# Sending expert outputs home by scatter instead of storing and gathering them, in a one-core attention and mixture-of-experts block

## The chip, the cores and the metric

The kernel runs on one core of a Trainium2 chip. The metric is the device time of one execution in microseconds, as a median over runs; less is better.

## What is computed

One transformer block over 4 x 1024 tokens of 128 features, all in float32. Its second half, a feed-forward with 16 experts of which each token uses one, beside a shared expert of 512 columns, is what the change touches.

```python
# x: (4, 1024, 128)
x = x + attention(layernorm(x))          # 16 heads of 8, no softmax: (q k^T / n^sigmoid(m)) v
h = layernorm(x).reshape(4096, 128)
logits = h @ router_w.T                  # 16 experts, top 1
score = sigmoid(top value), zero for the other experts
routed_in = h * score
gate, up = split(routed_in @ gate_up_proj[e])          # 128 -> 2 x 128
expert = (up * silu(gate)) @ down_proj[e]
shared = (silu(h @ shared_gate_w.T) * (h @ shared_up_w.T)) @ shared_down_w.T
x = x + shared + expert
```

## The kernel before

The 4096 tokens are 32 tiles of 128 rows; a group c is four of them (NQ = 8 groups). Token 128 t + p sits in partition p of tile t, in the residual `xres` and in the normed rows `h_rows`.

**Stages.** In the attention stage (`project`, `turn_q`, `v_by_k`, `attend` on TensorE) each group is projected, normed and added to the residual; `turn_h` and `route` give its router logits. On the vector engine `choose(c)` finds the top expert and `place(c)` the row of every token in the DRAM buffer `x_slots` (`pos`), in which each expert has a region with 128 rows of zeros ahead. GpSimd writes each tile's 128 rows there with an indirect DMA, `scatter(t)` (L353, issue at L358), 32 in all; a row is 128 features and the top logit, W = 129 words. When all are in, `slot_rows` and `take_table` make a table of 48 slots of 128 rows, each for one expert; slots that are not full reach into the zero rows or are not used.

**Expert stage**, in 12 groups g of four slots: SP loads the slots' rows (`load(g)`, L244, four DMAs at L251, first row from the table in registers); TensorE turns them (`turn_rows`), does gate and up (`gate_up_experts`), turns the product (`turn_act`) and does `down_experts`; ScalarE copies the result into the ring `yg` (`take_y`, L540, four buffers), and SP stores it to the DRAM buffer `y_slots` (`store(g)`, L253, issue at L255).

**The way back.** The vector engine works out where each token's y row lies (`y_rows`, L839 to L843, index `y_row`). When all twelve stores have landed, GpSimd gathers 32 tiles by that index into `h_rows` (L428 to L433), at most two under way (semaphores `back`). `add_experts(c)` (L858) waits for the four gathers of its group and for `add_shared(c)` and adds them to the residual (L863); SP stores the even groups and ScalarE's queue the odd ones (L285, L706).

**Shared expert.** 32 blocks n = 4 c + k of 128 of the 512 columns: `gate_up_shared(n)` (L1214, six matmuls, with `hT` split in a high and a low half), `silu_shared` on ScalarE (L517), `act_shared` on the vector engine (L850), `down_shared(n)` (L1224). The low half of group c is made on GpSimd by `hT_lo(c)` (L342, instruction at L344); block n waits for that of group n // 4 (`hT_rdy`, L1218). `add_shared(c)` adds a group's sum to the residual (L856).

**Order.** Every engine runs a list written out by hand, one call a line (SP from L258, GpSimd L361 to L433, ScalarE from L546, vector engine from L911, TensorE from L1278), and waits on semaphores in that order. TensorE's list mixes shared blocks into the expert stage: `gate_up_shared(10)` and `down_shared(9)` stand in it, and 11 to 31 follow it. On the vector engine the last calls are `add_shared(7)`, `add_experts(6)`, `add_experts(7)`.

Of the kernel before, what the change touches and what calls it, by code (L numbers as in the profile page):

```python
# [7 lines left out]
ALU = mybir.AluOpType  # L8
# [9 lines left out]
def build_block(nc, S, x, x_t, w_in, b_in, Wo, bo, m_col_in, router_t, gate_up, down, shared_gate, shared_up,  # L18
# [18 lines left out]
    W = D + 1  # L37
# [3 lines left out]
    YRING = 4  # L41
# [9 lines left out]
    y_slots = nc.dram_tensor("y_slots", (SLOTS * P, D), F32, kind="Internal").ap()  # L51

    with ExitStack() as ctx:
# [41 lines left out]
        from_slot = sb("from_slot", [P, NQ, Q])  # L95
        y_row = sb("y_row", [P, NT], I32)
# [56 lines left out]
        offs_all = sb("offs_all", [P, NQ, E, Q])  # L153
# [40 lines left out]
        y_st = [sem(f"y_st{i}") for i in range(YRING)]  # L194
        y_row_rdy = sem("y_row_rdy")
        back = [sem("back0"), sem("back1")]
# [6 lines left out]

        table_cols = table[:].rearrange("o a n -> o (a n)")
# [23 lines left out]
        def _(sp):  # L228
# [8 lines left out]
            sp.wait_ge(z_done, 1)  # L237
# [21 lines left out]
            load(0)  # L259
            load(1)  # L260
            load(2)
            load(3)
            load(4)
            load(5)
            load(6)
            load(7)
            load(8)
            store(0)
            store(1)
            load(9)  # L270
            store(2)
            load(10)
            load(11)
            store(3)
            store(4)
            store(5)
            store(6)
            store(7)
            store(8)
            store(9)  # L280
            store(10)
            store(11)
# [6 lines left out]
        def _(pool):  # L289
# [33 lines left out]
                   allow_small_or_imprecise_dtypes=True)  # L323
            g.iota(e_no[:], pattern=[[1, E]], base=0, channel_multiplier=0, allow_small_or_imprecise_dtypes=True)
# [3 lines left out]
                   allow_small_or_imprecise_dtypes=True).then_inc(k_ids, 1)  # L328

# [23 lines left out]
            def scatter(t):  # L353
                if t % Q == 0:
# [9 lines left out]
            scale_q(1)  # L364
            scale_q(2)
            scale_v(2)
            count(0)
            scale_v(3)
            scale_q(3)
            scatter(0)  # L370
            scatter(1)
            count(1)
            scatter(2)
            scatter(3)
            hT_lo(0)
            scale_v(4)
            scale_q(4)
            scatter(4)
            scale_v(5)
            scatter(5)  # L380
            scale_q(5)
            scatter(6)
            scatter(7)
            hT_lo(1)
            count(2)
            hT_lo(2)
            scale_v(6)
            scale_q(6)
            scatter(8)
            scatter(9)  # L390
# [3 lines left out]
            scatter(12)  # L394
            scatter(13)
            count(3)
            scatter(14)
            count(4)
            scatter(15)
            scale_q(7)  # L400
            scatter(16)
            scatter(17)
            scatter(18)
            scatter(19)
            hT_lo(3)
            scatter(20)
            scatter(21)
            count(5)
            scatter(22)
            scatter(23)  # L410
            count(6)
            scatter(24)
            scatter(25)
            scatter(26)
            scatter(27)
            count(7)
# [3 lines left out]
            scatter(31)  # L420
            hT_lo(4)
            hT_lo(5)
            hT_lo(6)
# [12 lines left out]
        def _(act):  # L436
# [103 lines left out]
            def take_y(g):  # L540
                act.wait_ge(e_dn_mm, g + 1)
                if g >= YRING:
                    act.wait_ge(y_st[g % YRING], 16 * (g // YRING))
# [3 lines left out]
            std_x(1)  # L547
            std_x(2)
            square(0)
            head_norms(0)  # L550
            square(1)
            weights_hi(0)
            std_x(3)
            weights_hi(1)
            head_norms(1)
            std_x(4)
            qT_copy(0)
            qT_copy(1)
            square(2)
            std_x(5)  # L560
            wb_copy(0)
            std_x(6)
            x1_copy(0)
            head_norms(2)
            std_h(0)
            norm_h(0)
            x1_copy(1)
            square(3)
            hT_copy(0)
            std_h(1)  # L570
            hT_hi(0)
            qT_copy(2)
            norm_h(1)
            head_norms(3)
            hT_copy(1)
            hT_hi(1)
            square(4)
            qT_copy(3)
            wb_copy(1)
            head_norms(4)  # L580
            x1_copy(2)
            square(5)
            std_h(2)
            head_norms(5)
            x1_copy(3)
            norm_h(2)
            std_h(3)
            hT_copy(2)
            qT_copy(4)
            hT_hi(2)  # L590
            std_x(7)
            norm_h(3)
            qT_copy(5)
            wb_copy(2)
            square(6)
            hT_copy(3)
            hT_hi(3)
            head_norms(6)
            x1_copy(4)
            square(7)  # L600
            silu_shared(0)
            silu_shared(1)
            std_h(4)
            head_norms(7)
            norm_h(4)
            x1_copy(5)
            hT_copy(4)
            hT_hi(4)
            std_h(5)
            silu_shared(2)  # L610
            qT_copy(6)
            wb_copy(3)
            silu_shared(3)
            norm_h(5)
            x1_copy(6)
            hT_copy(5)
            qT_copy(7)
            std_h(6)
            hT_hi(5)
            norm_h(6)  # L620
            x1_copy(7)
            hT_copy(6)
            hT_hi(6)
            std_h(7)
            norm_h(7)
            hT_copy(7)
            silu_shared(4)
            hT_hi(7)
            silu_shared(5)
            silu_shared(6)  # L630
            silu_shared(7)
            silu_shared(8)
            silu_shared(9)
            score_silu(0)
            rows_copy(0)
# [3 lines left out]
            score_silu(2)  # L639
            rows_copy(2)  # L640
            gate(1)
            score_silu(3)
            rows_copy(3)
            gate(2)
            take_y(0)
            score_silu(4)
            gate(3)
            score_silu(5)
            silu_shared(10)
            rows_copy(4)  # L650
            take_y(1)
            score_silu(6)
            rows_copy(5)
            score_silu(7)
            take_y(2)
            gate(4)
            score_silu(8)
            rows_copy(6)
            gate(5)
            take_y(3)  # L660
            rows_copy(7)
            score_silu(9)
            take_y(4)
            rows_copy(8)
            score_silu(10)
            gate(6)
            gate(7)
            take_y(5)
            score_silu(11)
            rows_copy(9)  # L670
            gate(8)
            take_y(6)
            rows_copy(10)
            gate(9)
            take_y(7)
            rows_copy(11)
            gate(10)
            gate(11)
            take_y(8)
            take_y(9)  # L680
            take_y(10)
            take_y(11)
            silu_shared(11)
            silu_shared(12)
# [24 lines left out]
        def _(dve):  # L709
# [129 lines left out]
            def y_rows():  # L839
                link(v.tensor_tensor(offs_all[:], hot[:], row_a[:].unsqueeze(1).unsqueeze(3).broadcast_to([P, NQ, E, Q]),  # L840
                                     ALU.mult))
                link(v.tensor_reduce(from_slot[:], offs_all[:].rearrange("p c e t -> p c t e"), AX.X, ALU.add))
                v.tensor_tensor(y_row[:], pos[:], from_slot[:].rearrange("p c t -> p (c t)"), ALU.subtract  # L843
                                ).then_inc(y_row_rdy, 1)

# [71 lines left out]
            scale_mask()  # L917
            x_scales(0)
            x_stats(1)
            take(0, 0)  # L920
            x_stats(2)
            take(0, 1)
            x_scales(1)
            x_scales(2)
# [576 lines left out]
```

## Time and profile before

| what | us |
|---|---|
| median of 3 runs | 222.6 (221.36 to 223.38) |
| the profiled execution, its own time | 222.22 |
| its span in the trace | 220.2 |
| TensorE busy | 191.8 |
| vector engine busy | 146.7 |
| ScalarE busy | 107.3 |
| GpSimd busy | 95.4 |

The profiled execution's own time is 2.0 us more than its span, which runs from the first to the last thing that the trace shows. Issuing a DMA is not counted as busy on SP and ScalarE; on GpSimd an indirect DMA is an instruction with a duration. Engines work in parallel, so their times do not add up to the span. Matmuls are pipelined.

### The profile page before, as it was taken

How to read it: one execution, taken by the hardware profiler on the slowest of the kernel's cores; microseconds unless marked ns; L12 is line 12 of the kernel's file. 1: busy time of each engine (PE TensorE's matmuls, PEld its weight loads, DVE VectorE, ACT ScalarE, POOL GpSimd, SP SyncE). 2: the span in 40 equal slices, each digit the busy share in tenths (PEclk: the TensorE clock that was granted, in tenths of full speed). 3: DMA queues.
4: the chain of work that ended last, by engine and by line, in shares of the span. 5: the costliest groups of instructions: out<-in, count | busy, mean ns of one | idle time of the engine just before them, and what ended most of it. 6: DMA issues, size and time to landing. Idle time of an engine off the chain costs nothing.

```text
span 220.2 us, 3766 instructions
## 1 busy us (share of the span) xinstructions
PE 191.8 (87%) x1126; PEld 154.5 (70%) x1126; DVE 146.7 (67%) x504; ACT 107.3 (49%) x236; POOL 95.4 (43%) x122
## 2 busy tenths in 40 slices
PE   0786699999999997899969998999899999999920
PEld 0342457676777875788847996898788888888820
DVE  3699999999999856868347767873614255343531
ACT  3336358647879888561325655656442222322200
POOL 6002503388868778765910000000006667456660
PEclk9999999999999999999999999999999999999985
DMA  5999992010100111111254467522241131203351
GB/s 165 322 388 215 163 417 100 1 36 13 38 13 26 36 45 44 48 36 39 65 109 106 96 165 158 151 74 69 71 123 39 48 95 60 75 25 95 98 176 60
DMA packets 22278, 22.57 MB, mean 103 GB/s; under 512 B 2802, under 2 KB 17396, under 8 KB 22004
## 3 DMA queue, kind: packets, MB, share of 16 engines
q1 hardware_dynamic: 19056, 16.75, 27.7%
q0 software_dynamic: 2048, 4.21, 6.9%
q10 hardware_dynamic: 1156, 1.39, 1.8%
q8 instruction: 9, 0.15, 0.3%
q14 instruction: 9, 0.07, 0.1%
HBM read 13.93 MB, written 8.41 MB: 101 GB/s over the span
## 4 chain that ended last, share of the span: by engine, by line
DMA 26%; PE 23%; DVE 21%; SPq 10%; issue 8%; ACT 4%; POOL 4%; ACTq 0%; POOLq 0%; DVEq 0%
DMA h_rows<-y_slots,y_row 19%; SPq L251 8%; DVE qkv L758 4%; DMA x_slots<-h_rows,pos 4%; DVE st L720 3%; PE bank L1274 3%; PE quad_banks L1255 3%; DVE ss L766 3%; DVE rn L771 2%; DMA w_qkv<-w_in 2%; POOL h_rows L431 2%; ACT h_rows L473 2%; PE bank L1159 2%; PE quad_banks L1125 2%; PE bank L1164 2%
## 5 line engine op out<-in xcount | busy, mean ns | idle before, releaser
L431 POOL DMA_INDIRECT h_rows<-y_slots,y_row x32 | 31.6, 986 | 72.4 <-DMA y_slots<-yg 54.9
L850 DVE TENSOR_TENSOR s_act<-quad_banks,sg_act 128x512 f32<-128x512 f32 x32 | 22.1, 689 | 31.4 <-PE bank L1232 18.3
L517 ACT ACTIVATE sg_act<-quad_banks 128x512 f32<-128x512 f32 x32 | 19.0, 598 | 43.6 <-PE quad_banks L1212 43.4
L358 POOL DMA_INDIRECT x_slots<-h_rows,pos x32 | 31.4, 980 | 11.7 <-issue 5.6
L1232 PEld LDWEIGHTS bank<-sdT,s_act 128*128 128x128 f32 x256 | 32.0, 191 | 2.3 <-issue 0.2
L1232 PE MATMUL bank<-sdT,s_act 128*128 128x128 f32 x256 | 33.2, 277 | 0.0
L334 POOL TENSOR_TENSOR qkv<-qkv,rn 128x512 f32<-128x512 f32 x16 | 17.3, 1096 | 28.3 <-DVE rn L771 28.2
L1125 PE MATMUL quad_banks<-w_c,xT 128*128 128x384 f32 x64 | 24.8, 521 | 2.0 <-DVE qkv L758 1.4
L1255 PE MATMUL quad_banks<-w_gu,xgT 128*128 x96 | 22.9, 383 | 0.8 <-ACT xgT L528 0.8
L1255 PEld LDWEIGHTS quad_banks<-w_gu,xgT 128*128 128x128 f32 x96 | 17.3, 190 | 3.5 <-issue 1.7
L1125 PEld LDWEIGHTS quad_banks<-w_c,xT 128*128 128x128 f32 x64 | 11.8, 203 | 11.0 <-issue 2.8
L536 ACT ACTIVATE eg_act<-quad_banks,esc 128x128 f32<-128x128 f32 x48 | 13.7, 371 | 8.9 <-PE quad_banks L1255 8.9
L758 DVE SCALAR_TENSOR_TENSOR qkv<-quad_banks,rs,b_qkv 128x384 f32<-128x384 f32 x32 | 17.7, 602 | 0.2 <-PE quad_banks L1125 0.2
L720 DVE BATCH_NORM_STATS2 st<-xres 128x6 f32<-128x128 f32 x64 | 13.7, 277 | 4.6 <-ACT xres L467 3.7
L885 DVE SCALAR_TENSOR_TENSOR e_act<-quad_banks,esc,eg_act 128x128 f32<-128x128 f32 x48 | 13.5, 344 | 4.0 <-ACT eg_act L536 3.9
L1210 PE MATMUL quad_banks<-hT,sgT 128*128 128x512 f32 x32 | 14.9, 465 | 0.2
L473 ACT ACTIVATE h_rows<-xres,nm,rs 128x128 f32<-128x128 f32 x32 | 13.2, 486 | 3.8 <-DVE nm L744 3.6
L1274 PE MATMUL bank<-w_dn,e_actT 128*128 x96 | 13.2, 280 | 2.1 <-DVE e_actT L894 1.3
L1274 PEld LDWEIGHTS bank<-w_dn,e_actT 128*128 128x128 f32 x96 | 12.0, 191 | 3.8 <-issue 3.5
L1212 PE MATMUL quad_banks<-hT,suT 128*128 128x512 f32 x32 | 12.6, 395 | 0.0
L1212 PE MATMUL quad_banks<-hT,sgT 128*128 128x512 f32 x32 | 12.6, 394 | 0.0
L1211 PE MATMUL quad_banks<-hT,suT 128*128 128x512 f32 x32 | 12.6, 394 | 0.0
(143 smaller groups left out, 359.4 us busy)
## 6 DMA issues: line engine op xcount, KB each, us to landing
xg<-x_slots SPq DMA_DIRECT2D x48, 64.5 KB, 2.0
y_slots<-yg SPq DMA_DIRECT2D x12, 256.0 KB, 2.3
xT<-x_t SPq DMA_DIRECT2D x8, 256.0 KB, 7.0
xres<-L_attn_x SPq DMA_DIRECT2D x8, 256.0 KB, 7.1
w_gu<-gate_up SPq DMA_DIRECT2D x1, 2048.0 KB, 14.3
x_slots<-zeros SPq DMA_DIRECT2D x1, 1032.0 KB, 16.9
w_dn<-down SPq DMA_DIRECT2D x1, 1024.0 KB, 15.8
out<-xres SPq DMA_DIRECT2D x4, 256.0 KB, 2.1
```

What stands on the lines that cost most here:

```text
L251: sp.dma_start(xg[:, g * Q + j, :], x_slots[bass.ds(first[j], P), :]).then_inc(xg_ld[g], 16)
L358: g.indirect_dma_start(out=x_slots, out_offset=bass.IndirectOffsetOnAxis(ap=pos[:, t:t + 1], axis=0), in_=h_rows[:, t, :], in_offset=None) ...
L431: g.indirect_dma_start(out=h_rows[:, t, 0:D], out_offset=None, in_=y_slots, in_offset=bass.IndirectOffsetOnAxis(ap=y_row[:, t:t + 1], axis ...
L517: a.activation(sg_act[:, n % 2], pair[:, 2 * (n % 2)], ACT.Silu).then_inc(s_silu, 1)
L720: last = v.bn_stats(st[:, t, :], xres[:, t, :])
L758: last = v.scalar_tensor_tensor(out=qkv[:, c % QRING, j, :], in0=pair[:, j, 0:QKV], scalar=rs1[:, t:t + 1], in1=b_qkv[:], op0=ALU.mult, op ...
L850: v.tensor_tensor(s_act[:, n % 2], pair[:, 2 * (n % 2) + 1], sg_act[:, n % 2], ALU.mult).then_inc(s_act_rdy, 1)
L1125: last = te.matmul(pair[:, j, 0:QKV], xT[:, P * (Q * c + j):P * (Q * c + j + 1)], w_c[:], start=True, stop=True)
L1212: return te.matmul(to, lhs[:, 1], rhs[:, 0], start=False, stop=True)
L1232: last = te.matmul(Y_BANK[c][:, here], s_act[:, n % 2, here], sdT[:, D * k:D * k + D], start=(k == 0 and j == 0), stop=(k == KC - 1 and j ...
L1255: mm = te.matmul(gate_up_banks(g % 2)[:, j, :], xgT[:, g % 2, P * j:P * j + P], gu_cols[:, bass.ds(held[g][j] * 2, F2)], start=True, stop= ...
L1274: mm = te.matmul(ps_yg[:, here], e_actT[:, g % 2, here], dn_cols[:, bass.ds(cols[j], D)], start=True, stop=True)
```

## The change

- A row of `x_slots` has a second extra word, an integer: the place of its token in the output order, p x 32 + t for token row p of tile t, filled into `h_rows` once at the start. In the zero rows it is 4096 and more.
- `y_slots` and the index computation `y_rows` are removed. `yg` has 12 buffers instead of 4.
- `send(g)` on GpSimd: for each of the four slots of group g, once its y is in `yg`, one indirect DMA scatters the 128 rows to `y_back` by the index that came with the rows; indices above 4095 are left out (`bounds_check`). 48 in all, at most three under way.
- `bring(c)` on SP: when all 48 have landed, eight plain loads bring `y_back` into the space of `h_rows`, four tiles each, 2 KB a partition. `add_experts(c)` waits for its load.
- The twelve `send` calls stand on GpSimd behind `scatter(31)`, `hT_lo(3)` and `hT_lo(4)`; `hT_lo(5)` comes behind `send(9)`, `hT_lo(6)` and `hT_lo(7)` behind `send(11)`. SP's list is all loads, then the eight `bring`, then the output stores.
- The lists of all engines are in a new order. On TensorE `gate_up_shared(2)` and `(3)` move behind `attend(7)`; `down_shared(8)` and `(9)` go to the first expert groups, `gate_up_shared(10)` and `(11)` to the middle, `down_shared(10)`, `gate_up_shared(12)` and `(13)` to the last four. On the vector engine `add_experts(0)` and `(1)` stand behind `act_shared(25)`, `(2)` behind 26, `(3)` to `(5)` behind 28, `(6)` ahead of and `(7)` behind `add_shared(7)`.

```diff
-    W = D + 1
+    W = D + 2
-    YRING = 4
+    YRING = 12
...
-    y_slots = nc.dram_tensor("y_slots", (SLOTS * P, D), F32, kind="Internal").ap()
+    y_back = nc.dram_tensor("y_back", (T, D), F32, kind="Internal").ap()
...
+        y_rows = h_rows[:].rearrange("p t w -> p (t w)")[:, 0:NT * D].rearrange("p (t d) -> p t d", d=D)
+        by_place = y_back[0:T, :].rearrange("(p t) d -> p t d", t=NT)
...
-            sp.wait_ge(z_done, 1)
+            sp.wait_ge(z_done, 2)
...
-            def store(g):
-                sp.wait_ge(yg_rdy, g + 1)
-                sp.dma_start(y_slots[g * Q * P:(g + 1) * Q * P, :].rearrange("(j p) d -> p j d", p=P), yg[:, g % YRING]
-                             ).then_inc(y_st[g % YRING], 16)
+            def bring(c):
+                if c == 0:
+                    for turn, landed in enumerate(y_sent):
+                        sp.wait_ge(landed, 16 * len(range(turn, SLOTS, 3)))
+                sp.dma_start(y_rows[:, Q * c:Q * c + Q, :], by_place[:, Q * c:Q * c + Q, :]).then_inc(y_ld[c], 16)
...
+            for g in range(NG):
+                load(g)
+            for c in range(NQ):
+                bring(c)
...
+            g.iota(h_rows[:, :, D + 1].bitcast(I32), pattern=[[1, NT]], base=0, channel_multiplier=NT)
...
+            pool.wait_ge(z_done, 1)
+            g.iota(zeros[:, :, D + 1].bitcast(I32), pattern=[[P, E]], base=T, channel_multiplier=1).then_inc(z_done, 1)
...
+            def send(g):
+                pool.wait_ge(yg_rdy, g + 1)
+                for j in range(Q):
+                    n = g * Q + j
+                    if n >= 3:
+                        pool.wait_ge(y_sent[n % 3], 16 * (n // 3))
+                    nc.gpsimd.indirect_dma_start(
+                        out=y_back, out_offset=bass.IndirectOffsetOnAxis(ap=xg[:, n, D + 1:D + 2].bitcast(I32), axis=0),
+                        in_=yg[:, g % YRING, j], in_offset=None, bounds_check=T - 1, oob_is_err=False).then_inc(y_sent[n % 3], 16)
...
-            for stored in y_st:
-                pool.wait_ge(stored, 16 * NG // YRING)
-            pool.wait_ge(y_row_rdy, 1)
-            for t in range(NT):
-                if t >= 2:
-                    pool.wait_ge(back[t % 2], 16 * (t // 2))
-                g.indirect_dma_start(out=h_rows[:, t, 0:D], out_offset=None, in_=y_slots,
-                                     in_offset=bass.IndirectOffsetOnAxis(ap=y_row[:, t:t + 1], axis=0)
-                                     ).then_inc(back[t % 2], 16)
...
             def add_experts(c):
-                for landed in back:
-                    dve.wait_ge(landed, 16 * (Q // 2) * (c + 1))
+                dve.wait_ge(y_ld[c], 16)
                 dve.wait_ge(y_free, c + 1)
                 r = xres[:, Q * c:Q * c + Q, :]
-                v.tensor_tensor(r, r, h_rows[:, Q * c:Q * c + Q, 0:D], ALU.add).then_inc(fin, 1)
+                v.tensor_tensor(r, r, y_rows[:, Q * c:Q * c + Q, :], ALU.add).then_inc(fin, 1)
```

## Rows read from the trace of the kernel before

**Rows 1.** The page, part 1: busy us, share of the span, instructions.

```profile
PE 191.8 (87%) x1126; PEld 154.5 (70%) x1126; DVE 146.7 (67%) x504; ACT 107.3 (49%) x236; POOL 95.4 (43%) x122
```

**Rows 2.** The chain that ended last, in order of time: start us, length us, what.

```profile
162.38 2.27 DMA y_slots<-yg
...
213.74 2.56 DMA h_rows<-y_slots,y_row
```

**Rows 3.** The vector engine's list, 210 us to the end: start us, us, engine, line, operation.

```profile
210.89 0.69 DVE L856 TENSOR_TENSOR xres<-bank,xres 128x512 f32<-128x512 f32 x1 [1.25 <-PE bank L1232]
211.50 0.68 DVE L863 TENSOR_TENSOR xres<-xres,h_rows 128x512 f32<-128x512 f32 x1
216.38 0.69 DVE L863 TENSOR_TENSOR xres<-xres,h_rows 128x512 f32<-128x512 f32 x1 [4.20 <-DMA h_rows<-y_slots,y_row]
```

**Rows 4.** Windows: from:to us, length, busy us (instructions) of each engine, granted clock, DMA share, GB/s.

```profile
0.00:20.00 20.00, 11.93 (x26) 5.45 (x26) 14.43 (x53) 8.00 (x14) 3.35 (x26) 1.00 0.90 289
...
110.00:120.00 10.00, 7.98 (x44) 6.08 (x44) 5.43 (x25) 4.93 (x17) 0.72 (x1) 1.00 0.51 107
...
130.00:140.00 10.00, 8.74 (x63) 7.88 (x62) 6.90 (x27) 5.74 (x17) 0.00 (x0) 1.00 0.72 172
...
150.00:160.00 10.00, 9.33 (x64) 8.07 (x63) 5.92 (x16) 4.99 (x14) 0.00 (x0) 1.00 0.26 75
...
161.00:211.00 50.00, 49.85 (x309) 43.99 (x307) 21.40 (x33) 13.14 (x22) 29.09 (x30) 1.00 0.28 80
```

**Rows 5.** GpSimd's list: scatters, low halves, gathers; in brackets the idle time before.

```profile
101.35 0.96 POOL L358 DMA_INDIRECT x_slots<-h_rows,pos  x1 [0.30 <-issue]
...
105.72 5.00 POOL L344 TENSOR_TENSOR hT<-hT_full,hT 128x512 fp32r<-128x512 f32 x4
165.57 0.99 POOL L431 DMA_INDIRECT h_rows<-y_slots,y_row  x1 [54.86 <-DMA y_slots<-yg]
...
174.07 0.95 POOL L431 DMA_INDIRECT h_rows<-y_slots,y_row  x1 [0.31 <-issue]
...
185.31 1.46 POOL L431 DMA_INDIRECT h_rows<-y_slots,y_row  x1 [0.38 <-DMA h_rows<-y_slots,y_row]
```

**Rows 6.** ScalarE's list: the first and the last of the twelve y copies.

```profile
122.31 0.60 ACT L544 COPY yg<-bank 128x512 f32<-128x512 f32 x1
...
161.77 0.59 ACT L544 COPY yg<-bank 128x512 f32<-128x512 f32 x1 [1.43 <-PE bank L1274]
```

**Rows 7.** L358's durations; landings of scatters, gathers, y stores; the opening loads.

```profile
L358 POOL DMA_INDIRECT x_slots<-h_rows,pos x32: 954/960/1175, 44.4 to 104.7; - x32
...
DMA to landing us min/median/max: 2.3/2.4/3.9
...
DMA to landing us min/median/max: 2.4/2.6/4.5
...
DMA to landing us min/median/max: 2.3/2.3/3.9
...
xres<-L_attn_x SPq DMA_DIRECT2D x8, 256.0 KB, 7.1
```

**Rows 8.** TensorE's list: the hole at 137.89, and gate-up block 24's first matmul.

```profile
137.89 1.15 PE L1274 MATMUL bank<-w_dn,e_actT 128*128 x8 [1.26 <-DVE e_actT L894]
...
190.34 0.48 PE L1210 MATMUL quad_banks<-hT,sgT 128*128 128x512 f32 x1
```

**Rows 9.** SP's list: the first two y stores.

```profile
129.66 0.97 SPq L255 DMA_DIRECT2D y_slots<-yg  x2
```

**Rows 10.** The vector engine's list: load 9 arrived, an addition, product 25.

```profile
135.10 0.17 DVE L868 TENSOR_TENSOR logit_inv<-xg 128x4 f32<-128x4 f32 x1 [1.36 <-DMA xg<-x_slots]
...
185.28 0.68 DVE L863 TENSOR_TENSOR xres<-xres,h_rows 128x512 f32<-128x512 f32 x1
...
195.82 0.69 DVE L850 TENSOR_TENSOR s_act<-quad_banks,sg_act 128x512 f32<-128x512 f32 x1 [1.33 <-ACT sg_act L517]
```

**Rows 11.** The vector engine's groups from 121 to 145 us: busy us, mean ns, idle before.

```profile
L872 DVE RECIPROCAL logit_inv<-logit 128x4 f32<-128x4 f32 x8 | 1.4, 178 | 0.3
```

More of the change, by code:

```diff
@@ L193, in build_block @@
         aT_mm, aT_sb, e_dn_mm, yg_rdy = sem("aT_mm"), sem("aT_sb"), sem("e_dn_mm"), sem("yg_rdy")
-        y_st = [sem(f"y_st{i}") for i in range(YRING)]
-        y_row_rdy = sem("y_row_rdy")
-        back = [sem("back0"), sem("back1")]
+        y_sent = [sem(f"y_sent{i}") for i in range(3)]
+        y_ld = [sem(f"y_ld{c}") for c in range(NQ)]
         fin, out_st = sem("fin"), sem("out_st")
@@ L364, in _ @@
             scale_q(1)
+            scale_v(2)
             scale_q(2)
-            scale_v(2)
-            count(0)
             scale_v(3)
             scale_q(3)
+            hT_lo(0)
+            count(0)
+            scale_v(4)
             scatter(0)
+            scale_q(4)
             scatter(1)
+            scatter(2)
             count(1)
-            scatter(2)
             scatter(3)
-            hT_lo(0)
-            scale_v(4)
-            scale_q(4)
             scatter(4)
-            scale_v(5)
             scatter(5)
             scale_q(5)
+            scale_v(5)
             scatter(6)
@@ L385, in _ @@
             count(2)
+            scale_v(6)
+            scatter(8)
             hT_lo(2)
-            scale_v(6)
+            scatter(9)
             scale_q(6)
-            scatter(8)
-            scatter(9)
             scatter(10)
@@ L394, in _ @@
             scatter(12)
+            count(3)
             scatter(13)
-            count(3)
+            scale_q(7)
             scatter(14)
+            scatter(15)
             count(4)
-            scatter(15)
-            scale_q(7)
             scatter(16)
@@ L542, in take_y @@
                 if g >= YRING:
-                    act.wait_ge(y_st[g % YRING], 16 * (g // YRING))
+                    for turn, landed in enumerate(y_sent):
+                        act.wait_ge(landed, 16 * len(range(turn, Q * (g - YRING + 1), 3)))
                 a.copy(yg[:, g % YRING], ps_yg[:].rearrange("p (j d) -> p j d", d=D)).then_inc(yg_rdy, 1)
@@ L592, in _ @@
+            qT_copy(5)
+            head_norms(6)
+            wb_copy(2)
             norm_h(3)
-            qT_copy(5)
-            wb_copy(2)
-            square(6)
+            x1_copy(4)
             hT_copy(3)
+            square(7)
+            head_norms(7)
+            std_h(4)
+            x1_copy(5)
+            norm_h(4)
             hT_hi(3)
-            head_norms(6)
-            x1_copy(4)
-            square(7)
+            hT_copy(4)
+            qT_copy(6)
+            std_h(5)
@@ L620, in _ @@
[L620 to L628, printed above, removed]
+            x1_copy(7)
+            norm_h(6)
+            std_h(7)
+            hT_copy(6)
+            norm_h(7)
+            silu_shared(2)
+            hT_copy(7)
+            silu_shared(3)
+            silu_shared(4)
+            hT_hi(5)
             silu_shared(5)
             silu_shared(6)
+            hT_hi(6)
@@ L917, in _ @@
             scale_mask()
+            x_stats(1)
             x_scales(0)
-            x_stats(1)
             take(0, 0)
+            x_scales(1)
+            take(0, 1)
             x_stats(2)
-            take(0, 1)
-            x_scales(1)
-            x_scales(2)
             take(1, 0)
@@ L1305, in _ @@
-            turn_q(3, after=(qT_sb, 3))
-            project(5, 1, after=(qkv_sb, 10))
             fold_wo(1)
             attend(2, after=(qT_sb, 4))
-            count_before(1)
+            turn_h(1, after=(hT_sb, 1))
+            count_before(0)
+            project(5, 1, after=(qkv_sb, 10))
+            route(1, after=(pos_rdy, 1))
             project(6, 0, after=(qkv_sb, 11))
             attend(3, after=(x1_rdy, 3))
+            count_before(1)
+            turn_q(4, after=(x1_rdy, 4))
@@ L1344, in _ @@
             count_before(5)
+            gate_up_shared(2, after=(s_act_rdy, 1))
             turn_h(6, after=(hT_sb, 6))
@@ L1389, in _ @@
             down_experts(3, after=(yg_rdy, 3))
+            turn_rows(7, after=(gT_sb, 7))
             turn_act(4, after=(aT_sb, 4))
[L1391 to L1392 removed]
+            gate_up_shared(10, after=(e_act_rdy, 5))
+            gate_up_shared(11, after=(e_act_rdy, 6))
             down_experts(4, after=(yg_rdy, 4))
```

435 lines of the change are left out of this document (201 added, 234 removed).

## The prediction

> **What bounds the kernel now.** I began with the page's busy shares [rows 1]. TensorE is busy 87% of the span and GpSimd 43%, but GpSimd's work lies in two blocks with 54.86 us of waiting between them, and the second begins at 165.57 [rows 5]. So two things compete for the end: TensorE's queue and GpSimd's second block. The chain that ended last [rows 2] says which: its last 54 us are the last y store (landing at 164.7), then one return gather after another, then one addition at 216.38. The vector engine's list at the end [rows 3] gives the price. The last shared addition starts at 210.89, right behind TensorE's last matmul; the addition of row group 6 follows at 211.50; then the vector engine stands idle for 4.20 us for the last gather and adds at 216.38. The output store of that group and the span's end follow 220.2 - 217.07 = 3.13 us after that addition ends (216.38 + 0.69).
>
> The windows [rows 4] say what is left under the gathers. Between 161 and 211 TensorE is busy 49.85 of 50 us at a granted clock of 1.00. So nothing that only touches the gathers can bring the end below TensorE's own end, 210.9. Before 161 it is not full: 8.1 us idle in the first 20, 2.0 in 110 to 120, 1.3 in 130 to 140, 0.7 in 150 to 160.
>
> **Part 1: the return gathers and y stores go.** The 32 gathers of 0.94 us, beginning at 165.57 and the last at 213.74, landing at 216.3 [rows 2, 5], leave, and so does their wait for all twelve stores. With them out of the way the tail is what follows TensorE: shared addition at 210.89, expert addition 0.61 us behind it and 0.68 long, so 212.18, plus the 3.13 us of store: 215.3. Against 220.2 that is 4.9 us, the whole that this part alone can give.
>
> **Part 2: 48 sends are added to GpSimd, earlier.** Each needs its y block; the first block is copied at 122.31 and ready at 122.9, the twelfth at 162.4 [rows 6], so blocks come every 3.6 us on average. The trace of before has no bounds-checked scatter, so its cost is bounded by neighbours. Two indirect DMAs in a row without a DMA wait start 1.25 us apart for gathers (0.95 + 0.31) and 1.28 for scatters into the same kind of memory (0.96 + 0.30) [rows 5]. The longest gather took 1.46, with 0.30 behind it 1.76. The mean pace of the 32 gathers, waits included, was (213.74 - 165.57) / 31 = 1.55. I take 1.28, the scatter's row, since a send is a scatter; the range keeps 1.25 and 1.76. Why no wait for landing in it: the gathers go two at a time, so a landing of 2.55 to 2.6 us from the start of the instruction [rows 7] is waited for at a pace of 1.28 (two make 2.56). The sends go three at a time, which allows 3 x 1.28 = 3.84 us; scatters land in a median of 2.4, and only the longest ones seen, 3.9 and 4.5, are above.
>
> At 1.28 four sends need 5.1 us a block against 3.6 for its making, so the queue is GpSimd's own almost from the start: the twelfth block waits for GpSimd and not the reverse. Sum: 122.9 + 48 x 1.28 = 184.3, plus one low-half subtraction of the hidden rows (L344) that now stands ahead of the last eight sends, 1.25 (four took 5.00 [rows 5]): 185.6. The last send starts at 184.3 and lands by 186.7 (2.4).
>
> **Part 3: what is queued behind the sends.** On GpSimd, the low halves of groups 6 and 7 stand behind the last send. Group 6's is done at 185.6 + 1.25 = 186.9. TensorE needs it for the gate-up block number 24, which started at 190.34 in the trace [rows 8]. So the cover is 3.4 us, and from that block to TensorE's end are 210.9 - 190.34 = 20.5 us of work. This, not the landing of y, is the tighter of the two. On SP the eight loads stand behind the last send's landing: 186.7 + about 0.1; a 256 KB store took 2.3 us and at most 3.9 [rows 7], so the first group is there at 189.2 to 190.7, and the slowest neighbour, the opening loads of the kernel at 7.1, would give 193.9. The first expert addition now stands behind product 25, which ran at 195.82 [rows 10]. The other seven loads need only 2 MB within 15 us. What stands behind a late addition on the vector engine is the next product, and TensorE behind that; at the nearer rows no one waits.
>
> **Part 4: TensorE's holes in the expert stage.** On SP the first two y stores stood ahead of load 9 at 129.66, for 0.97 us [rows 9], and without them that load goes out at least a microsecond earlier. In the trace the vector engine waited 1.36 us for its rows at 135.10, copied the turned activations behind them, and TensorE stood idle for 1.26 us until that copy [rows 8, 10]: recovered. The computation of the gathers' rows on the vector engine (L840 to L843) goes as well; I count nothing for it. The idle 2.0 us of 110 to 120 and the 0.7 of 150 to 160 [rows 4] now have shared work put between the waiting blocks: down blocks 8 and 9 go in behind the first gate-up of the experts, gate-up 12 and 13 and down 10 in the last four groups. I take half of the 2.0 us and all of the 0.7. Sum of part 4: 1.3 + 1.0 + 0.7 = 3.0, at least 0 and at most 3.9.
>
> **Part 5: the rest.** All queues are reordered in the attention stage. Two gate-up blocks (1.4 us each, six matmuls from 190.34 to 191.8) leave the stretch before the last attention tiles, which brings routing forward, but the chain there passes through four engines, and I take it as nothing, with 3 us either way. The two index fillings on GpSimd fall at 4 us, and GpSimd then idles until 20.46: free, and a row of 520 bytes in the scatters and loads is 0.8% more. The copies of y wait for nothing now, with twelve buffers: 0.
>
> One gather, at 185.31, took 1.46 us instead of 0.94, beside an addition of two SBUF tiles that began at 185.28 [rows 5, 10]. [...]
>
> **The sum.** TensorE ends at 210.9 - 3.0 = 207.9. Block 24 would then be wanted at 187.4, and part 3 has its input ready at 186.9: no stall, with 0.5 us to spare, which I hold for too little and so give 0.6 us back. TensorE's end 208.5, plus 0.03 + 0.61 + 0.68 + 3.13 = 4.45: span 212.95. The profiled execution took 222.22 around a span of 220.2, so 2.0 more: 215.0. It stood 0.4 under the median of 222.6, inside the spread of the runs, so I leave it at **215.0 us**, 3.4% less.
>
> **Rivals.** *The sends are slow and GpSimd's queue ends the kernel (slower).* With pace p the low half of group 6 is ready at 122.9 + 48p + 2.5 and the span ends 20.5 + 4.45 later: 150.4 + 48p. It reaches 212.95 at p = 1.30, 220.2 at 1.45, and from there the change loses. At the gathers' mean pace of 1.55 it is 224.8, or 226.8 us; at 1.76 it is 234.9, or 236.9. For it: the sends are bounds-checked, the pads' rows have to be sorted out, and nothing in the trace shows what that costs; 48 of them multiply every tenth by 5 us. Against: the fixed 0.94 to 0.96 of every indirect DMA, whatever its direction. Price taken: 228, chance 0.17.
>
> *Small vector operations hold up the sends.* Between 121 and 145 five kinds of 128x4 operations on SBUF alone run 8 times each for 0.16 to 0.18 us, 6.5 us in all (one kind's row is in [rows 11], the others are alike). If each stops GpSimd for its length, p rises for the first 20 sends and the total by up to 6.5: 150.4 + 61.4 + 6.5 = 218.3, or 220.3 us. [...] Against it: 32 scatters beside the vector engine's busiest stretch took 954 to 1175 ns, median 960 [rows 7]. Chance 0.11.
>
> *The reordered attention stage loses what the end wins.* If routing comes 3 us later everything behind does: 218 us. TensorE is idle 210.9 - 191.8 = 19 us before its end, all but 4 of it ahead of the expert stage [rows 1, 4], and that says this stage is a chain and not a full engine, so an order can cost as well as gain. Chance 0.08. *The loads from y_back are late:* at 7.1 us a load the first addition is asked for at 195.8 - 2.4 and gets its rows at 193.9: 0.5 us. Held inside the forecast.
>
> **How the numbers follow.** Forecast 0.64 with its own range 211.5 to 218; slow sends 0.17, lock 0.11, attention stage 0.08. A measurement here tells about 1% from no change, 2.2 us. Faster by over 1% (under 220.4) takes the forecast (0.64), the attention rival (0.08) and a quarter of the lock (0.03): 0.75; within 1% fall the rest of the lock (0.08) and the cheap end of the slow sends (0.02): 0.10; slower is the rest of the slow sends: 0.15. The range goes from 211.0 (attention stage and holes both give) to 222.5, leaving the slow sends outside.
>
> **What would show it.** Right: indirect DMAs of 0.94 to 1.0 us, 1.25 to 1.3 apart, from about 122 to 186 without a DMA wait between them; TensorE at its end between 206 and 211 with no hole before block 24; the last expert addition right behind the last shared one, the 4.20 us gone; the hole of 1.26 at 137.9 gone. Wrong: sends over 1.1 us long or over 1.35 apart; TensorE waiting for L344 (on GpSimd) at some 187 to 195, or the vector engine for the y_back loads at its first expert addition.

## The result and the profile after

The changed kernel takes 215.8 us (median of 4 runs, 214.1 to 217.6) against 222.8 for the kernel before (4 runs): ratio 0.969, interval 0.962 to 0.975. The forecast was 215.0. Run again later it took 216.4 against 221.9, ratio 0.974 (0.968 to 0.980). Some executions of a kernel take over 1.5% more than its fastest one: the medians here are over all executions, the ratios and their intervals leave those out. The profiled execution took 214.33 us around a span of 212.6; forecast were 215.0 and 212.95.

GpSimd's list of the changed kernel, with the idle time ahead in brackets: the first sends, a long landing's wait, the low half among the sends, the last send, and the low halves of groups 6 and 7.

```profile
122.57 1.01 POOL L352 DMA_INDIRECT y_back<-yg,xg  x1 [15.02 <-ACT yg L543]
123.89 0.99 POOL L352 DMA_INDIRECT y_back<-yg,xg  x1 [0.30 <-issue]
...
156.13 0.98 POOL L352 DMA_INDIRECT y_back<-yg,xg  x1 [1.39 <-DMA y_back<-yg,xg]
...
175.15 1.33 POOL L327 TENSOR_TENSOR hT<-hT_full,hT 128x512 fp32r<-128x512 f32 x1
...
185.68 0.98 POOL L352 DMA_INDIRECT y_back<-yg,xg  x1 [0.30 <-issue]
186.67 2.54 POOL L327 TENSOR_TENSOR hT<-hT_full,hT 128x512 fp32r<-128x512 f32 x2
```

These take the place of the gathers in [rows 5]. A send, bounds check and left-out rows included, is 0.98 us, with 0.30 behind it: a pace of 1.29 where a scatter's was 1.28. The first begins at 122.57, 0.8 us after its y copy ended, and the last at 185.68. Only one wait is long, 1.39 us at 156.13. The same lines as one group, with the landings, and the eight loads:

```profile
L352 POOL DMA_INDIRECT y_back<-yg,xg x48: 981/984/1010, 122.6 to 185.7; - x48
L255 SPq DMA_DIRECT2D h_rows<-y_back x8: 332/432/1359, 187.9 to 192.0; - x8
...
DMA to landing us min/median/max: 2.1/2.3/5.8
```

```profile
DMA to landing us min/median/max: 3.0/5.0/5.8
```

The sends (first answer) last 981 to 1010 ns, though the vector engine's small operations ran beside them all the while. The first answer goes by the tensor and has the loads in it: its 5.8 is a load's. The loads (second answer) land after 3.0 to 5.8 us. The first is the one that takes 3.0; the later ones take longer, while the DMA engines are busy 0.78 of the time between 190 and 192 us and 0.86 between 192 and 194.

TensorE's list, at gate-up block 24, and the vector engine's from the first expert additions to the end:

```profile
188.02 0.50 PE L1200 MATMUL quad_banks<-hT,sgT 128*128 128x512 f32 x1 [0.22 <-POOL hT L327]
```

```profile
192.96 0.69 DVE L842 TENSOR_TENSOR s_act<-quad_banks,sg_act 128x512 f32<-128x512 f32 x1 [1.58 <-PE bank L1222]
193.56 1.28 DVE L854 TENSOR_TENSOR xres<-xres,h_rows 128x512 f32<-128x512 f32 x2
...
207.28 0.68 DVE L854 TENSOR_TENSOR xres<-xres,h_rows 128x512 f32<-128x512 f32 x1
208.61 0.69 DVE L848 TENSOR_TENSOR xres<-bank,xres 128x512 f32<-128x512 f32 x1 [0.65 <-PE bank L1222]
209.40 0.69 DVE L854 TENSOR_TENSOR xres<-xres,h_rows 128x512 f32<-128x512 f32 x1
```

Block 24 waits 0.22 us for its low half: the 3.4 us that the forecast had between that low half and the start of block 24 in [rows 8] are just used up. The first expert additions follow product 25 without a gap, so their rows were there. At the end the addition of group 7 stands right behind the shared one; the 4.20 us of [rows 3] are gone. TensorE's last matmul ends at 208.58 (forecast 208.5), and the span 4.0 us later (forecast 4.45).

Last, where TensorE's idle time went. Windows of the attention stage, the expert stage and the shared tail, columns as in [rows 4]; before, then after:

```profile
0.00:107.00 107.00, 92.02 (x500) 67.02 (x501) 89.10 (x342) 65.11 (x128) 60.17 (x88) 1.00 0.38 112
107.00:163.00 56.00, 51.90 (x333) 45.21 (x332) 34.34 (x127) 29.61 (x87) 3.72 (x4) 1.00 0.45 109
163.00:211.00 48.00, 47.85 (x297) 42.26 (x295) 21.40 (x33) 12.55 (x21) 29.09 (x30) 1.00 0.27 78
```

```profile
0.00:107.00 107.00, 93.27 (x492) 66.99 (x492) 89.17 (x340) 62.04 (x127) 60.39 (x89) 1.00 0.38 112
107.00:163.00 56.00, 53.49 (x353) 48.56 (x352) 35.30 (x128) 29.32 (x87) 30.53 (x32) 1.00 0.36 86
```

Idle in the first window: 15.0 us before, 13.7 after; in the second 4.1 and 2.5. The first difference cannot be put down to the change: the four traces of kernels with the old lists and the old way back (`before` and three of the experiments below) have TensorE busy from 91.8 to 93.0 us up to 107, and the traces with the new lists 92.3 to 93.3.

### The profile page after: what moved, and what is told of

It is laid out like the page before. It is cut to its first block, busy times and chain, and to the rows that moved or that the text cites. A ratio compares the mean times of both kernels' runs of the same rounds, so it can differ in the third digit from the quotient of the medians.

```text
span 212.6 us, 3825 instructions
## 1 busy us (share of the span) xinstructions
PE 192.1 (90%) x1126; PEld 155.6 (73%) x1126; DVE 146.2 (69%) x501; ACT 103.2 (49%) x234; POOL 112.1 (53%) x140
## 3 DMA queue, kind: packets, MB, share of 16 engines
q10 hardware_dynamic: 1156, 1.39, 1.9%
## 4 chain that ended last, share of the span: by engine, by line
PE 29%; DVE 28%; POOL 16%; issue 12%; DMA 8%; ACT 5%; POOLq 1%; ACTq 0%; DVEq 0%
POOL y_back L352 14%; PE bank L1222 8%; DVE qkv L757 7%; DMA y_back<-yg,xg 6%; DVE ss L765 4%; DVE st L719 4%; PE quad_banks L1200 3%; PE quad_banks L1202 3%; PE quad_banks L1201 3%; PE quad_banks L1115 3%; ACT h_rows L471 2%; DVE rn L770 2%; DMA w_qkv<-w_in 2%; PE quad_banks L1245 2%; DVE mv L722 2%
## 5 line engine op out<-in xcount | busy, mean ns | idle before, releaser
L352 POOL DMA_INDIRECT y_back<-yg,xg x48 | 47.3, 985 | 30.5 <-ACT yg L543 15.0
L1115 PE MATMUL quad_banks<-w_c,xT 128*128 128x384 f32 x64 | 25.9, 544 | 2.0 <-DVE qkv L757 1.2
L1115 PEld LDWEIGHTS quad_banks<-w_c,xT 128*128 128x128 f32 x64 | 12.6, 212 | 11.3 <-issue 4.4
L534 ACT ACTIVATE eg_act<-quad_banks,esc 128x128 f32<-128x128 f32 x48 | 13.7, 371 | 9.7 <-PE quad_banks L1245 8.9
L719 DVE BATCH_NORM_STATS2 st<-xres 128x6 f32<-128x128 f32 x64 | 13.7, 276 | 1.4 <-DMA xres<-L_attn_x 1.4
L885 DVE COPY e_actT<-bank 128x512 f32<-128x512 f32 x12 | 8.3, 689 | 8.2 <-PE bank L1253 7.1
L327 POOL TENSOR_TENSOR hT<-hT_full,hT 128x512 fp32r<-128x512 f32 x8 | 10.7, 1356 | 3.8 <-ACT hT L481 3.7
L1264 PE MATMUL bank<-w_dn,e_actT 128*128 x96 | 12.6, 275 | 0.0
```

Of the source, the lines that this page charges most:

```text
L352: nc.gpsimd.indirect_dma_start(out=y_back, out_offset=bass.IndirectOffsetOnAxis(ap=xg[:, n, D + 1:D + 2].bitcast(I32), axis=0), in_=yg[:, ...
L719: last = v.bn_stats(st[:, t, :], xres[:, t, :])
L1115: last = te.matmul(pair[:, j, 0:QKV], xT[:, P * (Q * c + j):P * (Q * c + j + 1)], w_c[:], start=True, stop=True)
L1264: mm = te.matmul(ps_yg[:, here], e_actT[:, g % 2, here], dn_cols[:, bass.ds(cols[j], D)], start=True, stop=True)
```

## The experiments

Each ratio is to runs of the kernel before beside it on the same chip; where the text says "changed kernel" in a ratio it is the 0.974 of `after_again`, unless it says otherwise.

**1. The way back without the order, and the order without the way back.** The two halves of the change, each alone.

```diff
# old_order_new_way: the kernel before with x_slots rows of D + 2, y_back, send, bring, YRING = 12,
# expert additions behind products 25 to 28; all other calls in the order of before
-            load(0) ... store(11)
+            for g in range(NG):
+                load(g)
+            for c in range(NQ):
+                bring(c)
...
             hT_lo(7)
-            for t in range(NT):
-                g.indirect_dma_start(out=h_rows[:, t, 0:D], ...)
+            send(0) ... send(11)
```

> The sends, the eight loads, twelve y buffers and the late expert additions, but the engines' lists of the kernel before (low halves all ahead of the sends). Theory: the gain is the gathers' tail plus the hole of 1.26 us that the stores on SP made; TensorE ends at about 209.6 instead of 210.9, the span is 213.6 and the time about 215.5, within 1% of the changed kernel. Rival (the order is what frees the sends' time): without it the gather tail alone goes and nothing else, 217.3 or more, and the vector engine waits at the first expert addition.

Measured: 216.2 us against 221.3, ratio 0.977 (0.972 to 0.982); span 212.4. The same as the changed kernel within the intervals (0.969 and 0.974 in its two runs).

```diff
# new_order_old_way: the changed kernel's lists, with y_slots, store, y_rows and the return gathers of before,
# SP's list of before, all low halves ahead of the gathers, expert additions spread among the products as before
-            send(0) ... send(11)
+            for t in range(NT):
+                if t >= 2:
+                    pool.wait_ge(back[t % 2], 16 * (t // 2))
+                g.indirect_dma_start(out=h_rows[:, t, 0:D], ...)
```

> The new lists with the y stores and return gathers of the kernel before (expert additions at the places of before). Theory: the gathers again set the end; in the new lists the last y copy comes at 164.1 instead of 161.8, so the span is about 222 and the time 223 to 225, no gain or a small loss against before. Rival (the order carries the gain): 218 to 220.

Measured: 227.4 us against 221.3, ratio 1.027 (1.022 to 1.033), worse than even the theory had it. GpSimd's first and last gather and the vector engine's last addition:

```profile
169.28 0.99 POOL L437 DMA_INDIRECT h_rows<-y_slots,y_row  x1 [57.35 <-DMA y_slots<-yg]
...
218.16 0.95 POOL L437 DMA_INDIRECT h_rows<-y_slots,y_row  x1 [1.07 <-DMA h_rows<-y_slots,y_row]
```

```profile
220.86 0.69 DVE L869 TENSOR_TENSOR xres<-xres,h_rows 128x512 f32<-128x512 f32 x1 [5.85 <-DMA h_rows<-y_slots,y_row]
```

The gathers start 3.7 us later than in [rows 5], since three gate-up blocks more stand ahead of the last y block, and the vector engine waits 12.5 us for them in all. So the new order loses 6.1 us with the old way back (by the profiled executions' spans 4.4: 224.6 against 220.2), and with the new way it neither gains nor loses anything that the measurement can tell (0.974 to 0.969 with it, 0.977 without): all of the change's gain comes with the new way back. That way brings two things at once, the sends and a third DMA under way; experiments 4 and 5 take them apart.

**2. What stands behind the sends.**

```diff
# low_early
             hT_lo(4)
+            hT_lo(5)
+            hT_lo(6)
+            hT_lo(7)
             send(0)
...
             send(9)
-            hT_lo(5)
             send(10)
             send(11)
-            hT_lo(6)
-            hT_lo(7)
```

> The changed kernel with the low halves of groups 5 to 7 ahead of the first send, where GpSimd idles 15 us. Theory: what is queued behind the sends costs next to nothing, since TensorE waited 0.22 us for it: 0 to 0.5 us less than the changed kernel. Rival (the sends are the bound of the whole, as the chain of the changed kernel has them): 1.3 us or more less.

Measured: 214.2 us against 221.3, ratio 0.970 (0.964 to 0.976); span 212.3, TensorE's end at 208.3 instead of 208.6. No difference that the measurement can tell, as the theory had it. The chain that ended last puts 14% of the changed kernel's span on the sends, but all that TensorE waits for behind them is 0.22 us.

```diff
# tail_swap: as low_early, and (with the semaphores that go with it)
-            add_shared(7)
-            add_experts(7)
+            add_experts(7)
+            add_shared(7)
```

> As low_early, and the last group's expert rows are added before its shared sum, so that one addition and not two stands behind TensorE's last matmul. Theory: the tail behind TensorE's end is a chain, so 0.6 to 0.8 us less than low_early. Rival (the output store's queue sets the end): no difference.

Measured: 213.8 us, ratio 0.965 (0.960 to 0.970). From the end of TensorE's last matmul to the end of the span it is 3.3 us (208.2 to 211.5) against 4.0 in low_early: the 0.7 expected. The times differ by 0.4, inside their intervals.

**3. The price of a slower send.** A fill of a spare tile stands ahead of each send.

```diff
# slow_sends
+                    if n >= 1:
+                        pool.wait_ge(lag, n)
+                    g.memset(scrap[:], 0.0).then_inc(lag, 1)
                     nc.gpsimd.indirect_dma_start(
```

> Each send has a GpSimd fill of 128x256 ahead of it and a wait for it, some 0.4 to 0.5 us, so the pace goes from 1.29 to about 1.75. Theory (low half of group 6 is ready at 122.6 + 48p + 2.6, and 20.5 + 4.0 us of work follow): span 149.7 + 48p, 233.7 at 1.75; TensorE waits for the low halves. Rival (the sends have slack of their own under TensorE): under 220.

Measured: 224.7 us against 221.5, ratio 1.018 (1.009 to 1.027), span 223.6. The fill took 0.34 us and stood in place of part of the gap of 0.30, so the pace rose only to 1.47, 1.50 with the waits, and not to 1.75. GpSimd's last send, TensorE's blocks 20 and 24, and windows of TensorE (length, busy, granted clock, DMA share, GB/s):

```profile
195.06 0.98 POOL L357 DMA_INDIRECT y_back<-yg,xg  x1 [0.17 <-issue]
196.06 2.52 POOL L329 TENSOR_TENSOR hT<-hT_full,hT 128x512 fp32r<-128x512 f32 x2
```

```profile
184.36 0.79 PE L1205 MATMUL quad_banks<-hT,sgT 128*128 128x512 f32 x1 [5.22 <-POOL hT L329]
...
197.40 0.51 PE L1205 MATMUL quad_banks<-hT,sgT 128*128 128x512 f32 x1 [2.08 <-POOL hT L329]
```

```profile
190.00:195.00 5.00, 5.00 (x31) 1.00 0.01 0
195.00:197.00 2.00, 0.32 (x3) 1.00 0.05 9
197.00:199.00 2.00, 1.60 (x5) 0.74 0.15 29
199.00:201.00 2.00, 2.00 (x10) 0.50 0.93 286
201.00:203.00 2.00, 2.00 (x11) 0.90 1.00 319
```

TensorE waits twice: 5.22 us at block 20, for the low half that stands between the sends, and 2.08 us at block 24. The low half of block 24 is ready at 197.4. The formula at a pace of 1.50 from a first send at 123.4 gives 123.4 + 72.0 + 2.6 = 198.0. From there TensorE needed 22.2 us to its end (219.6) and not 20.5. It had stood idle from 195.3 to 197.4, and the granted clock of the three windows from 197 to 203 was 0.74, 0.50 (1.2 instead of 2.4 GHz) and 0.90: what is missing to 1.00, over 2 us each, is 1.7 us in all (0.52 + 1.00 + 0.20). So the slow rival of the prediction is a real mechanism, and a stall costs more than its length; that the clock is what the 1.7 us are is this sum, no run took it away. The whole span is 0.7 us over the formula's (223.6 against 198.0 + 20.5 + 4.45 = 222.95), since the low half came 0.6 earlier and less followed TensorE's end. The loss at 1.50 is 3.2 us, or 0.07 a send over 48 sends, so that the break-even, an estimate from this one point and not run, lies near 1.43.

**4. Two sends under way instead of three.**

```diff
# two_under_way
-        y_sent = [sem(f"y_sent{i}") for i in range(3)]
+        y_sent = [sem(f"y_sent{i}") for i in range(2)]
...
-                    if n >= 3:
-                        pool.wait_ge(y_sent[n % 3], 16 * (n // 3))
+                    if n >= 2:
+                        pool.wait_ge(y_sent[n % 2], 16 * (n // 2))
```

> Two sends under way instead of three. If the pace of 1.29 rests on the landing of a scatter, 2.3 us, being shorter than two instructions, 2.57, the pace stays under 1.33 and the time within 1.5 us of the changed kernel. If it rests on the third semaphore, the pace goes towards the gathers' 1.55 and the time up by 8 to 12 us.

Measured: 229.8 us, ratio 1.038 (1.030 to 1.046), slower than the kernel before. GpSimd's list, and TensorE at block 20:

```profile
148.50 0.98 POOL L352 DMA_INDIRECT y_back<-yg,xg  x1 [0.73 <-DMA y_back<-yg,xg]
149.80 0.98 POOL L352 DMA_INDIRECT y_back<-yg,xg  x1 [0.32 <-issue]
151.52 0.98 POOL L352 DMA_INDIRECT y_back<-yg,xg  x1 [0.73 <-issue]
152.81 0.98 POOL L352 DMA_INDIRECT y_back<-yg,xg  x1 [0.31 <-issue]
...
202.96 2.54 POOL L327 TENSOR_TENSOR hT<-hT_full,hT 128x512 fp32r<-128x512 f32 x2
```

```profile
191.83 0.80 PE L1200 MATMUL quad_banks<-hT,sgT 128*128 128x512 f32 x1 [11.75 <-POOL hT L327]
```

```profile
DMA to landing us min/median/max: 2.1/2.3/6.1
```

The median landing is 2.3 us as in the changed kernel (the 6.1 again is a load's), but a send that waits for it starts 3.02 us after the one it waits for (148.50 to 151.52): it lands after 2.2, and 0.8 pass until the next begins. The old gathers wait less behind a landing. In the chain of the kernel before:

```profile
182.52 2.53 DMA h_rows<-y_slots,y_row
```

This gather lands at 185.05, and the next begins at 185.31 [rows 5], 0.26 later and 2.8 after the one it waits for. Two under way therefore cannot keep the pace of 1.29 or 1.25: a start 3.0 or 2.8 us behind the last but one makes 1.5 or 1.4 us a DMA, and single long landings (up to 4.4 and 4.5) make most of the rest. The pace here is (202.0 - 123.9) / 47 = 1.66, where the changed kernel's by the same division is 1.34, each with one low half inside. TensorE waits 11.75 us at block 20, for the low half that stands ahead of `send(10)`. So the depth carries 13 us of this kernel's time, and my reading of "landing" as the time until the next may start was wrong.

**5. Depth in the kernel before.** If the third semaphore does this for the sends, what does it do for the old gathers?

```diff
# gathers_three: the kernel before, and
-        back = [sem("back0"), sem("back1")]
+        back = [sem(f"back{i}") for i in range(3)]
...
-                if t >= 2:
-                    pool.wait_ge(back[t % 2], 16 * (t // 2))
+                if t >= 3:
+                    pool.wait_ge(back[t % 3], 16 * (t // 3))
```

> The kernel before with three return gathers under way instead of two, and nothing else. Two sends under way ran at 1.6 us a piece and three at 1.29. If the depth and not the direction made the old tail, the gathers go at 1.25 to 1.3, end near 207 to 209, TensorE sets the end, the 4.2 us wait goes: about 217 us, ratio 0.975 to 0.985. If the scatter way is what counts, the gathers keep 1.5 or more and the time stays within 1 us.

Measured: 217.8 us against 221.9, ratio 0.983 (0.978 to 0.988); span 214.4. GpSimd's gathers and the vector engine's end:

```profile
164.69 0.99 POOL L431 DMA_INDIRECT h_rows<-y_slots,y_row  x1 [54.04 <-DMA y_slots<-yg]
...
168.50 0.94 POOL L431 DMA_INDIRECT h_rows<-y_slots,y_row  x1 [0.30 <-issue]
```

```profile
L431 POOL DMA_INDIRECT h_rows<-y_slots,y_row x32: 940/944/1134, 164.7 to 203.8; - x32
```

```profile
209.98 0.69 DVE L856 TENSOR_TENSOR xres<-bank,xres 128x512 f32<-128x512 f32 x1 [1.25 <-PE bank L1232]
210.59 1.28 DVE L863 TENSOR_TENSOR xres<-xres,h_rows 128x512 f32<-128x512 f32 x2
```

The gathers go 1.25 us apart without a wait, the last begins at 203.8 instead of 213.74, and the last two expert additions stand right behind the shared one. The tail is gone without a send.

```diff
# gathers_three_loads_first: as gathers_three, and
-    YRING = 4
+    YRING = 12
...
-            load(0) ... store(11)
+            for g in range(NG):
+                load(g)
+            for g in range(NG):
+                store(g)
```

> The same with all slot loads ahead of the y stores on SP and twelve y buffers. If the changed kernel's gain is only these two things, this is as fast as it: within 0.5% of after_again. If the way of the rows counts for itself, it stays 1% or more behind.

Measured: 216.7 us against 221.9, ratio 0.978 (0.973 to 0.983), beside the unaltered changed kernel:

> The changed kernel unaltered, on the chip and in the rounds of the next three: 0.965 to 0.975 of the kernel before. It is the yardstick for them.

Measured: 216.4 us, ratio 0.974 (0.968 to 0.980). The difference of 0.3 us is inside both intervals: the old way back, with one semaphore more and the loads first, is as fast as the sends as far as the measurement can tell. The hole alone:

> The kernel before with all slot loads ahead of the y stores on SP and twelve y buffers, nothing else. Theory: TensorE's hole of 1.26 us at 137.9 goes, the last y store lands 1 to 1.3 us sooner and with it the gather chain: 221.2 to 221.8 against 222.8. Rival: the hole is the row computation's or moves elsewhere: no change.

(The kernel before with only the loads ahead of the stores and twelve buffers.) Measured: 220.1 us against 221.5, ratio 0.989 (0.981 to 0.997): some 1% less, which agrees with the 1.3 us of the hole, though the interval reaches from 0.3 to 1.9%. In its trace, of an execution of 221.5 us, TensorE has no hole near 137.9, though the row computation on the vector engine is still there, and it is busy 53.0 us between 107 and 163, where it was 51.9 before.

**6. Large vector operations beside the sends.** If the vector engine can hold GpSimd up, as beside the gather at 185.31 [rows 5, 10], large additions of SBUF tiles will show it. Five additions of two SBUF tiles that nothing needs, behind products 15 to 19.

```diff
# sbuf_adds
+                if 15 <= n < 20:
+                    dve.wait_ge(ld_wd, 16)
+                    v.tensor_tensor(spare[:, n - 15], w_dn[:, 0:Q], w_dn[:, Q:2 * Q], ALU.add)
```

> The changed kernel with five extra vector additions of two 128x512 SBUF tiles behind products 15 to 19, while sends run (0.68 us each, the result is not used). Port lock: each send that such an addition meets takes up to 0.6 us longer, so five of 1.1 to 1.6 us among sends that otherwise take 0.98. No lock: all stay at 0.98 to 1.01.

Measured, in one run: span 213.7. The vector engine's additions, then GpSimd's list at the same time:

```profile
172.65 0.68 DVE L847 TENSOR_TENSOR spare<-w_dn 128x512 f32<-128x512 f32 x1
...
175.50 1.85 DVE L847 TENSOR_TENSOR spare<-w_dn 128x512 f32<-128x512 f32 x1
...
178.48 0.68 DVE L847 TENSOR_TENSOR spare<-w_dn 128x512 f32<-128x512 f32 x1
```

```profile
171.44 1.02 POOL L353 DMA_INDIRECT y_back<-yg,xg  x1 [0.31 <-DMA y_back<-yg,xg]
172.76 1.42 POOL L353 DMA_INDIRECT y_back<-yg,xg  x1 [0.30 <-DMA y_back<-yg,xg]
174.49 0.98 POOL L353 DMA_INDIRECT y_back<-yg,xg  x1 [0.30 <-issue]
175.48 1.32 POOL L328 TENSOR_TENSOR hT<-hT_full,hT 128x512 fp32r<-128x512 f32 x1
176.96 1.27 POOL L353 DMA_INDIRECT y_back<-yg,xg  x1 [0.17 <-issue]
178.53 1.48 POOL L353 DMA_INDIRECT y_back<-yg,xg  x1 [0.30 <-issue]
180.31 0.98 POOL L353 DMA_INDIRECT y_back<-yg,xg  x1 [0.31 <-issue]
```

Three sends take 1.27 to 1.48 us, each begun while an addition ran, and the others 0.98 to 1.02. The addition at 175.50, begun just behind GpSimd's subtraction at 175.48, takes 1.85 us instead of 0.68. The other four take 0.68, also those at 170.92 and 179.68 that began while a send was already under way, and the send of 170.15 kept its 0.98. So a send is held up by an addition that it finds running, a subtraction on GpSimd holds up the addition, and a send holds up nothing here. For the subtraction this is what the Trainium skill says in "SBUF — State Buffer", section "SBUF: two separate sides": the port pair that the vector engine and GpSimd share is an exclusive lock, taken by a vector operation with two SBUF inputs against a GpSimd operation that reads SBUF, and who comes second waits out the other's instruction. The trace agrees: the subtraction lasts until 176.80 and the addition ends 0.55 us later. That the same lock holds up the sends is argued and not shown, since no row shows what a send reads.

The kernel before has it too, three times and not once as the prediction read it: the gathers at 185.31, 200.68 and 205.67 took 1.46, 1.25 and 1.42 us beside expert additions begun at 185.28, 200.43 and 205.59, while the gather at 179.71, begun ahead of an addition at 179.87, took 0.94.

**7. Four under way.** tail_swap with a fourth semaphore for the sends.

> tail_swap with four sends under way. Three under way left one wait of 1.39 us behind a long landing and otherwise none, and TensorE does not wait for the sends once the low halves are early: within 0.3 us of tail_swap, 1 to 1.5 us below after_again. If the sends' end matters, another 1 us less.

Measured: 214.1 us against 221.9, ratio 0.967 (0.963 to 0.971), the same as tail_swap's 0.965. One further execution of it took 389.4 us, with TensorE busy 374 us for the same 1126 instructions, which take 192 in the changed kernel; the ratio leaves it out, and its cause is open.

## Why the prediction was right, step by step

- **Part 1, the tail.** The 4.20 us of wait went, and expert addition 7 came right behind the shared one. What was wrong is what it was ascribed to. The prediction treated the gathers' end as a property of the way back and took the whole of it as this change's gain. gathers_three has the same tail with the old way back: one more semaphore gives 4.1 us of the 5.5 that the changed kernel gives beside it, and with the loads first as well it gives 5.2 of them.
- **Part 2, the pace.** 1.28 forecast, 1.29 measured; last send forecast at 184.3, and it began at 185.68, late by the one wait of 1.39 us that the forecast had not. Its reason had a wrong step: "a landing of 2.55 to 2.6 us ... is waited for at a pace of 1.28 (two make 2.56)". A dependent send starts 3.0 us after the one it waits for, so that two under way cannot go faster than 1.5 and came to 1.66 in all. Three allow 3.84 us and cover it. The value was right because the depth was three, not because scatters land sooner than gathers.
- **Part 3, what is queued behind.** The tighter place was named rightly: block 24 needed at 187.4, its input ready at 186.9 by forecast; it was ready at 187.9, and the block started at 188.02 after a wait of 0.22. The loads of y_back were forecast from a single 256 KB store, 2.3 to 3.9 us; the first took 3.0, inside that, and the others up to 5.8. They had room, since the first was issued at 187.86 and asked for at 193.56. Not seen was that a slower queue stalls first and longest at block 20, through the low half ahead of `send(10)`: 5.22 us in slow_sends, 11.75 in two_under_way.
- **Part 4, the holes.** The term 3.0 was too large: the idle time of the expert stage fell by 1.6 us (4.1 to 2.5). The hole at 137.9 went, by the loads, as old_loads_first has it; the shared blocks put between the waits filled the rest only in part, and new holes came, 0.80 at 127.2 among them. **Part 5** had the attention stage at nothing, and in this trace it gave 1.3. No run puts it down to the order, so it is the scatter between executions, and luck: old_order_new_way, with the old order, has TensorE busy 93.1 us up to 107, the changed kernel 93.3, low_early, with the new one, 92.7, and gathers_three, which changes nothing there, 93.0 against the 92.0 of the kernel before. The two misses cancel: TensorE's end went from 210.9 to 208.58, 2.3 us, where 2.4 was forecast.
- **The rivals.** The slow queue did not come, but slow_sends shows its mechanism, with a loss of 1.8% at a pace of 1.50. The holding up by small vector operations did not come: 981 to 1010 ns. By large ones it is real: 1.27 to 1.48 us in sbuf_adds. The attention stage did not lose.

## What to carry to other kernels

Count how many DMAs of a chain are under way before you replace the chain: a third semaphore alone took the old gathers from 1.55 to 1.26 us a piece, and that alone was worth most of this change (4.1 of 5.5 us). Judge the depth by how far apart a waiting DMA and the one it waits for start, here 3.0 us for sends and 2.8 for gathers, and not by the landing in the trace, 2.3 and 2.6. Then look at what is queued behind the new work on its engine, at each place and not only the last, and move it ahead where the engine idles.

## What was not expected

- A send that waits for another starts 0.7 to 0.9 us after that one's landing in two_under_way, a gather of the kernel before only 0.2 to 0.4. So it is not a price of every DMA that GpSimd issues. What makes the difference no run here tells; the first send of the changed kernel too starts 0.8 us after the copy that it waits for.
- Bounds checking and leaving out rows cost at most 0.02 us a DMA (0.98 against 0.96 for the scatters, which have the same 0.96 with the longer rows of the changed kernel).
- A stall of TensorE costs more than its length: after 2.08 us of it the granted clock was 0.74, 0.50 and 0.90 for 2 us each, 1.7 us more. Behind the hole of 1.26 us in the kernel before it stayed at 1.00.
- The fastest version run is tail_swap: 213.8 us, 0.965 of the kernel before. It beats that one surely; the changed kernel, 0.969 and 0.974 in its two comparisons, it beats by less than the intervals tell.
